# Newton rounds of the query and key norms on GpSimd instead of VectorE, in a fused linear-attention and local-attention network on one core

## What is computed

```python
def attn_layer(x, Wqkv, qs, ksc, Wo):          # 16 heads of 64, windows of 32 tokens
    q, k, v = split(x @ Wqkv)
    q = l2norm(q) * qs                         # t / max(norm(t), 1e-12), for each token and head
    k = l2norm(k) * ksc
    q = q * cos * scale + rotate_half(q) * sin * scale
    k = k * cos * inv + rotate_half(k) * sin * inv
    out = local_attention(q, k, v)             # softmax over the window before and this one
    return out @ Wo
...
for i in range(6):
    x = attn_layer(shift_tokens(x), ...) + x
    x = ffn_layer(shift_tokens(x), ...) + x    # layer norm, W1, gelu gate, W2
```

## Time and profile before

| | |
|---|---|
| median of three runs | 4097.17 us |
| lowest, highest | 4088.42, 4102.23 us |
| span of the profiled execution, first to last instruction | 4091.2 us |
| mean granted TensorE clock | 0.931 of full speed |
| PE busy | 3424.9 us (84%) |
| DVE busy | 3354.0 us (82%) |
| ACT busy | 3114.5 us (76%) |
| POOL busy | 2097.8 us (51%) |

### The profile page before, as it was taken

One profiled execution on the slowest core, in us unless ns is written; L12 is line 12 of the kernel. 1 busy time (PEld: TensorE's weight loads), 2 busy tenths in 40 slices (PEclk: granted clock), 3 DMA queues, 4 the chain that ended last, 5 costly groups with the idle time before them and its releaser, 6 DMA issues. The chain is left out here.

```text
span 4091.2 us, 121860 instructions
## 1 busy us (share of the span) xinstructions
PE 3424.9 (84%) x40924; PEld 2264.8 (55%) x40924; DVE 3354.0 (82%) x6043; ACT 3114.5 (76%) x9641; POOL 2097.8 (51%) x2534
## 2 busy tenths in 40 slices
PE   5688987788989679988688888877899867988977
PEld 4455555655555555555465555555555545555555
DVE  7798997489999569999659989856899966999975
ACT  3488897378998459988638888846889954998883
POOL 3455554455555345555445555534555544555544
PEclk8799998899999889999889999988999988999998
DMA  2000000100000100000100000010000010000001
GB/s 61 10 4 4 4 4 25 27 6 4 4 4 3 43 12 4 4 4 4 31 21 5 4 4 4 2 43 11 4 4 4 4 36 17 4 4 4 4 24 42
DMA packets 109598, 51.94 MB, mean 13 GB/s; under 512 B 62726, under 2 KB 106628, under 8 KB 108420
## 3 DMA queue, kind: packets, MB, share of 16 engines
q1 hardware_dynamic: 109444, 49.99, 4.9%
HBM read 22.57 MB, written 2.10 MB: 6 GB/s over the span
## 5 line engine op out<-in xcount | busy, mean ns | idle before, releaser
L1365 ACT ACTIVATE probs<-s_ps,nbias,rnorm 128x64 f32<-128x64 f32 x3072 | 1209.2, 412 | 92.3 <-DVE nbias L1058 82.7
L1570 POOL TENSOR_TENSOR qk_rot<-by_cos,by_sin 128x512 f32<-128x512 f32 x384 | 487.7, 1270 | 629.1 <-DVE by_sin L995 629.1
L604 PE MATMUL ring<-wvo,xsT 128*32 128x512 f32 x6144 | 776.5, 625 | 1.5 <-ACT qT L1173 1.0
L1557 POOL TENSOR_TENSOR probs<-probs,rrow 128x256 f32<-128x256 f32 x768 | 454.5, 613 | 565.7 <-DVE rrow L984 565.7
L1365 ACT ACTIVATION_READ_ACCUMULATOR probs<-s_ps,nbias,rnorm 128x1 f32 x3072 | 649.5, 211 | 0.0
L539 PE MATMUL qk_ps<-wqk_hi,xsT_hi 128*128 128x512 f32 x756 | 342.9, 454 | 333.8 <-DVE xsT_lo L974 333.8
L1351 ACT ACTIVATE squares<-qk_ps 128x1024 f32<-128x1024 f32 x378 | 386.1, 1021 | 222.6 <-PE qk_ps L541 222.0
L1580 POOL TENSOR_TENSOR qk_rot<-qk_rot,rnorm 128x1024 f32<-128x1024 f32 x192 | 365.3, 1902 | 361.6 <-DVE rnorm L739 361.6
L1007 DVE TENSOR_REDUCE sumsq<-squares 128x16 f32<-128x1024 f32 x384 | 464.0, 1210 | 82.8 <-ACT squares L1351 82.8
L553 PEld LDWEIGHTS ring<-cst,qk_rot 128*128 128x128 f32 x3072 | 372.1, 147 | 286.1 <-issue 216.9
L995 DVE TENSOR_TENSOR by_cos<-qk_ps,rotary 128x1024 f32<-128x1024 f32 x378 | 460.5, 1218 | 84.4 <-ACT squares L1351 54.0
(11 more groups left out here) (166 smaller groups left out, 6427.7 us busy)
## 6 DMA issues: line engine op xcount, KB each, us to landing
xs<-x_tok SPq DMA_DIRECT2D x194, 64.0 KB, 1.9
qk_rot<-L_ffn_Wqkv SPq DMA_DIRECT2D x7, 1024.0 KB, 6.5
by_cos<-x_tok SPq DMA_DIRECT2D x48, 128.0 KB
by_cos<-x_tok SPq DMA_DIRECT2D x48, 127.0 KB
wv<-L_ffn_Wqkv SPq DMA_DIRECT2D x7, 512.0 KB, 8.4
wo_pad<-L_ffn_Wo SPq DMA_DIRECT2D x14, 256.0 KB, 7.7
x_keep<-L_attn_x SPq DMA_DIRECT2D x4, 512.0 KB, 4.9
out<-x_keep SPq DMA_DIRECT2D x4, 512.0 KB, 4.5
```

What stands on the lines that cost most here:

```text
L604: last = mm(r[WIN * mh:WIN * (mh + 1), :], xsT[:, a, WIN * w:WIN * (w + 1)], wvo[:, mh, :, :], start=True, stop=True)
L1365: last = nc.scalar.activation(probs[:, a, h // 4, :, h % 4, :], s_ps[:, half, c:c + 2 * WIN].rearrange("p (s c) -> p s c", s=2), ACT.Exp, ...
L1557: last = g.tensor_tensor(p, p, r, ALU.mult)
L1570: g.tensor_tensor(d[:, :, lo], cs[:, :, lo], sn[:, :, hi], ALU.add)
```

## The change

The clamp and the seed stay on DVE, now one right after the other in a function `seeds`, which stands ahead of the maxima of the first half and of the keys' rotation. The clamp also multiplies by 0.5, since the rounds work with half the sum of squares, and the seed's constant takes that into account. The nine operations of the Newton rounds leave DVE. On POOL, `inverse_norms` makes three rounds of four operations of 128x32 at the head of a step, ahead of `normalise_k`, each waiting for the one before by the semaphore `rnormed`. What waited for `norm_step` waits for `rnormed`. The sums of squares of a tile wait for the rounds of the tile before, since these read `sumsq`. The seed waits in addition for the exponentials of two tiles before.

```diff
@@ DVE
-            def rsqrt(y, src, t, h, first, steps, base):
-                ops = [
-                    first,
-                    lambda: v.tensor_scalar(y.bitcast(I32), src.bitcast(I32), -0.5, RSQRT_MAGIC, ALU.mult, ALU.add),
-                ]
-                for _ in range(3):
-                    ops += [
-                        lambda: v.tensor_tensor(t, y, y, ALU.mult),
-                        lambda: v.scalar_tensor_tensor(h, t, -0.5, src, ALU.mult, ALU.mult),
-                        lambda: v.scalar_tensor_tensor(y, h, 1.5, y, ALU.add, ALU.mult),
-                    ]
...
                     def sum_of_squares(qk, s):
...
+                        dve.wait_ge(rnormed, passed(NEWTON_OPS * T))
                         dve.wait_ge(squared[qk], done(T))
...
-                    def inverse_norms(i0, i1, s):
+                    def seeds(s):
...
-                        if i0 <= 1 < i1:
-                            dve.wait_ge(k_rotated, done(T - 2))
-                        op = rsqrt(rnorm[:, a, :], sumsq[:, :], rs_t[:, :], rs_h[:, :],
-                                   lambda: v.tensor_scalar(sumsq[:, :], sumsq[:, :], 1e-24, None, ALU.max),
-                                   norm_step, RSQRT_OPS * T)
-                        for i in range(i0, i1):
-                            op(i)
+                        dve.wait_ge(summed["q"], done(T))
+                        dve.wait_ge(summed["k"], done(T))
+                        v.tensor_scalar(sumsq[:, :], sumsq[:, :], 1e-24, 0.5, ALU.max, ALU.mult).then_inc(halved, 1)
+                        for half in range(2):
+                            dve.wait_ge(exp_done[half], done(T - 2))
+                        dve.wait_ge(k_rotated, done(T - 2))
+                        dve.wait_ge(halved, done(T))
+                        v.tensor_scalar(rnorm[:, a, :].bitcast(I32), sumsq[:, :].bitcast(I32), -0.5,
+                                        RSQRT_MAGIC - 2 ** 22, ALU.mult, ALU.add).then_inc(seeded, 1)
...
-                    inverse_norms(3, 4, 1)
                     if it is not None or k != 1:
                         xsT_lower(0)
-                    inverse_norms(4, 5, 1)
                     maxima(1, 2)
-                    inverse_norms(5, 6, 1)
                     residual(3)
-                    inverse_norms(6, 8, 1)
                     softmax_bias(1, 2)
-                    inverse_norms(8, 9, 1)
                     row_reciprocals(0, 2)
-                    inverse_norms(9, 11, 1)
                     rotate("q", 0, 0)
...
                     sum_of_squares("k", 0)
+                    seeds(0)
                     maxima(0, 1)
-                    inverse_norms(0, 1, 0)
                     softmax_bias(0, 1)
-                    inverse_norms(1, 2, 0)
                     rotate("k", 0, 0)
-                    inverse_norms(2, 3, 0)
                     rotate("k", 1, 0)
@@ POOL
+                    def inverse_norms(s):
...
+                        ops = newton_on(rnorm[:, a, :], sumsq[:, :], rs_t[:, :], three_halves[:, :])
+                        for i, op in enumerate(ops):
+                            if i == 0:
+                                pool.wait_ge(seeded, done(T))
+                            else:
+                                pool.wait_ge(rnormed, passed(NEWTON_OPS * T + i))
+                            op().then_inc(rnormed, 1)
...
                         pool.wait_ge(added["k"], done(T))
-                        pool.wait_ge(norm_step, RSQRT_OPS * T + RSQRT_OPS)
+                        pool.wait_ge(rnormed, passed(NEWTON_OPS * T + NEWTON_OPS))
...
+                    inverse_norms(1)
                     normalise_k(1)
                     normalise(0, 2)
```

More of the change, by code:

```diff
@@ L54 @@
 RSQRT_MAGIC = 1597463007.0
-RSQRT_OPS = 11
 NEWTON_OPS = 12
@@ L164, in build @@
         rs_t = sb("rs_t", [P, 2 * H])
-        rs_h = sb("rs_h", [P, 2 * H])
         rnorm = sb("rnorm", [P, 2, 2 * H])
@@ L178, in build @@
         ln_rs = sb("ln_rs", [P, 2, 5, FT])
-        three_halves = sb("three_halves", [P, FT])
+        three_halves = sb("three_halves", [P, 2 * H])
         xnT = sb("xnT", [P, FT * P])
@@ L245, in build @@
             {qk: tile_sem(f"{qk}_{n}") for qk in "qk"} for n in ("projected", "squared", "summed", "read", "added")]
-        norm_step = sem("norm_step")
+        halved, seeded, rnormed = [tile_sem(n) for n in ("halved", "seeded", "rnormed")]
         k_rotated = tile_sem("k_rotated")
@@ L1015, in inverse_norms @@
                         T, a = T0 - s, (par - s) % 2
-                        if i0 == 0:
-                            dve.wait_ge(summed["q"], done(T))
-                            dve.wait_ge(summed["k"], done(T))
-                        if i0 <= 1 < i1:
-                            dve.wait_ge(k_rotated, done(T - 2))
-                        op = rsqrt(rnorm[:, a, :], sumsq[:, :], rs_t[:, :], rs_h[:, :],
-                                   lambda: v.tensor_scalar(sumsq[:, :], sumsq[:, :], 1e-24, None, ALU.max),
-                                   norm_step, RSQRT_OPS * T)
-                        for i in range(i0, i1):
-                            op(i)
+                        dve.wait_ge(summed["q"], done(T))
[7 more added lines that the diff above has]
+                                        RSQRT_MAGIC - 2 ** 22, ALU.mult, ALU.add).then_inc(seeded, 1)
                     def carry(s):
@@ L1055, in softmax_bias @@
                         dve.wait_ge(exp_done[half], done(T - 1))
-                        dve.wait_ge(norm_step, RSQRT_OPS * T + RSQRT_OPS)
+                        dve.wait_ge(rnormed, passed(NEWTON_OPS * T + NEWTON_OPS))
                         dve.wait_ge(max_done[half], done(T))
@@ L1474, in _, with newton, newton_on @@
             g.memset(vo[:, 2 * NW - 1, :], 0.0).then_inc(zeroed, 1)
-            def newton(rs, three_halves=three_halves[:, :]):
+            def newton(rs, three_halves=three_halves[:, 0:FT]):
                 _, half_var, y, t, _ = (rs[:, i, :] for i in range(5))
+                return newton_on(y, half_var, t, three_halves)
+            def newton_on(y, half_var, t, three_halves):
                 ops = [
@@ L1571, in add_rotated @@
                         g.tensor_tensor(d[:, :, hi], cs[:, :, hi], sn[:, :, lo], ALU.add).then_inc(added[qk], 1)
+                    def inverse_norms(s):
+                        if not there(k, it, s):
+                            return
+                        T, a = T0 - s, (par - s) % 2
+                        ops = newton_on(rnorm[:, a, :], sumsq[:, :], rs_t[:, :], three_halves[:, :])
[5 more added lines that the diff above has]
+                            op().then_inc(rnormed, 1)
                     def normalise_k(s):
@@ L1603, in _ @@
                 both = newton(ln_rs[:, :, :, :].rearrange("p a i t -> p i a t"),
-                              three_halves[:, :].unsqueeze(1).broadcast_to([P, 2, FT]))
+                              three_halves[:, 0:FT].unsqueeze(1).broadcast_to([P, 2, FT]))
                 for i, op in enumerate(both):
```

## The result

The changed kernel takes 4457.9 us (median of four runs, 4455.7 to 4459.7), beside 4097.7 us for the kernel before on the same chip. The ratio is 1.088, with a 95% interval of 1.085 to 1.091: 8.8% slower. The forecast was 4417 us, slower, with a range of 4190 to 4510.

The account below looks back on a forecast made before the run. No engine alone was taken as the bound; a loop through POOL, PE, ACT and DVE set the pace. 180 x 1.71 = 308 us plus 12 on 4091.2 gave 4411 of span, 6 more 4417 us; range 4190 to 4510.

Parts of the forecast that it names:

- The loop: From keys' rotation through POOL, PE, ACT and DVE to the next keys' rotation: 18.49 us a tile, against 16.78.
- The price of an operation: POOL's twelve chained 128x32 operations: 0.345 us each taken, 4.14 us a tile, bounds 3.31 to 4.62.
- The seed's wait: On DVE, the seed held until POOL's queries' sum ends, to 15.31 us; maxima and bias behind it cost 0.68 + about 0.15.
- the pace of the kernel before: Interval between `normalise_k` of successive tiles before the change: 503.48 / 30 = 16.78 us a tile.
- the sum of 320: Added span over six layers: 308 us from 180 steady intervals of 1.71 us, and 12 us at layers' ends.
- the layers' ends: Last tile of each layer late by what POOL's idle time doesn't hide: 6 x 2.02 = 12 us.
- The other paths fit inside: Query projection, queries' rotation, values, transposed queries and queries' squares fit within the 18.49 us tile; new wait costs nothing.
- first rival: POOL's queries' sum doesn't meet clamp and seed on DVE: 16.98 us a tile, 4145 us; not or partly held, chance 0.12.
- DVE's relief decides: Rival at the step's head: bias and ACT's exponentials come sooner, at most 83 us, 4014 us; faster, chance 0.07.
- Its condition: DVE's relief decides only if POOL's chain fits in 2.12 us, 0.18 us an operation, so transposed keys aren't late.
- DVE down by 500 us: Expected sign on DVE: its busy time down by some 500 us, and DVE idle before the keys' squares.
- PE's wait for `normalise_k`: Expected sign: PE's idle time in L553, released by POOL's `qk_rot`, 1 to 2 us a tile.

Follow-up runs that it names:

- The experiment with the old order: Changed kernel with DVE's order of before (maxima, clamp, bias, seed), rounds still between keys' sum and `normalise_k`: 4291.0 us, ratio 1.048 to the kernel before.
- the kernel with both moves: Changed kernel with rounds between POOL's queries' sum and keys' sum, and DVE's order maxima, clamp, bias, seed: 3929.0 us, ratio 0.960 to the kernel before.

## Why the prediction was right, step by step

Times from the end of the keys' rotation of one tile, in the tile shown above (zero is 515.03 + 1.21 = 516.24):

| step | predicted | measured |
|---|---|---|
| keys' sum through | 2.71 | 2.72 |
| rounds | 4.14 long | 3.92 long |
| `normalise_k` through | 8.76 | 8.50 |
| key projection through | 11.04 | 10.67 |
| keys' squares summed | 13.40 | 13.22 |
| queries' sum on POOL through | 15.27 | 15.05 |
| seed through | 15.31 | 15.09 |
| keys' rotation begins | 16.05 | 15.98 |
| one tile | 18.49 | 18.34 (mean 18.38) |

- **The loop** was right in mechanism and place, and in its size to 0.1 us. POOL's idle time ahead of `normalise_k` is gone (361.6 us in the kernel before, 15.0 now).
- **The price of an operation** was bounded from 0.276 to 0.385 us; it is 3.92 / 12 = 0.327. The 128x4 chain plus 28 columns at the 1.6 ns a column of the earlier trace rows would have given 0.321, nearer than the pace of the 128x8 chain that I took. The 2.6 cycles an element of the Trainium skill (GPSIMD Engine Reference, "3.1 Elementwise — side-by-side cycle accounting"), put on the 128x4 chain, would give 0.337, as an estimate, 3% above what was measured. The 128x8 chain was the wrong base: its pace of 0.345 is above that of 32 columns, so width is not what made it slow.
- **The seed's wait** was right: held until 0.04 us after POOL's queries' sum, with maxima and bias behind it. The experiment with the old order measures it at 0.89 us a tile, where I had 0.83.
- **What failed by size** is the pace of the kernel before. I took 16.78 us from 30 intervals of the first layer; over six layers it is 16.52. That makes 0.26 x 186 = 48 us, the largest of the corrections that together make the 45 us by which the sum of 320 fell short of 364.8. The other corrections: 18.38 for 18.49 is -20 us, 186 intervals in place of 180 are +10, and the layers' ends 18.5 us in place of 12. Why one layer was no measure shows in the windows of the kernel before: beside the earlier trace rows, with a granted clock of 0.94, stands

```profile
480.00:600.00 120.00, 108.84 (x1514) 69.10 (x1515) 111.08 (x202) 108.57 (x353) 68.35 (x67) 0.99 0.01 4
```

  with 0.99, where `normalise_k` comes at 491.38, 507.35 and 523.05, 15.7 to 16.0 us apart; in the window of the earlier trace rows the intervals are 16.5 to 17.6 us. The layers follow the clock too: with 0.96 over the attention of a layer it takes 518.8 us, with 0.97 508 to 511, with 0.98 506.9. Which of the two drives the other these rows do not say. The changed kernel has one pace in all layers at a clock of 0.94; that hardly any of its loop is PE's (2.2 of 18.4 us) would explain it, but was not tested.
- **"The other paths fit inside"** was true of the outcome and hid a fact. I counted the query projection's loop as it was. The run without rounds shows it at 17.08 us in the changed order, so about a third of the change's loss (3.2 of 8.8%) would have remained had POOL's chain cost nothing. The prediction's first rival, with the seed not held, had the pace 16.98 with no word of this second loop. PE's clock did not rise with more gaps, as I thought it may: it is 0.918 over the program, 0.931 before, and 0.94 in the attention, 0.96 to 0.98 before.
- **The rival "DVE's relief decides"** did not come true in the changed kernel, and without any rounds at all, in the old order, the relief gave 40 us. Its condition was right, that the chain must not make the transposed keys late; moved between the two sums it does not. But the kernel with both moves is then 154 us faster, where the rival's price was 83 at most, and not through ACT's waits for biases, which it priced: these are 78.5 us there and were 82.7. Most of that gain comes with the keys' sum moving away from `xsT_lo`.
- **Signs that did not come.** I expected DVE down by 500 us; it fell by 278. The removed operations overlap their neighbours in the records by about 0.1 us each (501.21 + 0.18 against the next start at 501.31), and part of their time was being held, which has moved: the seed's group grew from 72.5 to 199.9 us. PE's wait for `normalise_k` is 175.2 us in 96 cases for 192 tiles, not 1 to 2 us in each. In the tile shown above PE was still at the queries' transposes, which began at 524.23, when `normalise_k` ended at 524.74.

## What to carry to other kernels

Before work is moved to an idle engine, look for where on that engine's queue the idle time lies and which side of it the loop passes: with the old order of the seed, the same twelve operations gave a ratio of 1.048 on one side of the keys' sum and of 0.960 on the other. A busy share of 82% over the span, and 89% inside the attention, does not make an engine the bound: leaving all its removable work out was worth 40 of 553 us. And an order changed in passing (here clamp and seed ahead of the maxima) is a change of its own, to be priced alone: it cost 232 us on the old kernel. A gain has to be priced alone as well: most of the 4% of the good placement came with a POOL operation that was shifted and no longer held one on DVE; the work that left DVE gave 1.1% without that shift.

## What the runs showed of the hardware

- A chain of dependent POOL operations of 128x32, each with its own semaphore wait, runs at 0.327 us an operation while the records give it 0.24 to 0.26; chains of 128x4 run at 0.276 and of 128x8 (two rows of four) at 0.345. Why the last is slower was not tried.
- Two costs seen in one place can have different causes, and need not add up. The order of DVE alone and the chain alone cost 232 and 224 us on the old kernel, both together, in the changed kernel, 360. The chain lengthens the loop over POOL; the order lengthens this loop and that of the query projection. In the changed kernel the longer one counts, 18.38 us a tile; the other stands at 17.08 when the chain is gone.
- Where POOL and DVE execute side by side, some DVE operations are held until the POOL operation ends: the seed takes 0.17 us free and up to 1.23 held, `xsT_lo` 0.28 and 1.17 (kernel before). The products with the rotary tables, which have one input in PSUM, were never held: all 756 take 1.21 to 1.23 us.
- The clock granted to PE was 0.50 in the 2.8 us behind an idle gap of 2.6 us, which turned a projection of 1.6 us into one of 2.9 us. In the kernel without rounds such a gap stands in each tile (2.62 us on average, 192 of them) and the clock is 1.00 from 240 to 600 us, so the gap alone does not bring it down.
